# Six gate projections of a retention layer done in the kernel's opening

## The reference

```
mod = (silu(c) @ wmod).reshape(8, 6, 1, 128)
sa, ca, ga, sb, cb, gb = (mod[:, n] for n in range(6))
ga, gb = (sign(a) * maximum(abs(a), 0.25) for a in (ga, gb))
h = layernorm(x) * (1 + ca) + sa
q, k = rotary(h @ Wq.T), rotary(h @ Wk.T)
v, g = h @ Wv.T, h @ Wg.T
o = (q @ k.T / 8 * decay_causal) @ v
o = norm_by_head(o) * gn_weight + gn_bias
x = x + ga * ((o * silu(g)) @ Wo.T)
h = layernorm(x) * (1 + cb) + sb
r = sigmoid(mix(h, mu_r) @ W_r.T)
x = x + gb * r * (relu(mix(h, mu_k) @ W_k.T) ** 2 @ W_v.T)
```

## Time and profile before

| | us |
|---|---|
| median of 3 runs | 756.68 |
| lowest, highest | 756.54, 758.75 |
| span of the profiled execution | 754.3 |
| TensorE busy | 737.0 (98%) |
| VectorE busy | 605.7 (80%) |
| GpSimd busy | 586.0 (78%) |
| ScalarE busy | 489.5 (65%) |

### The profile page before, as it was taken

How to read it: one execution, slowest core, us unless ns; L and a number is a source line. 1 busy time by engine, 2 the same in 40 slices (tenths; PEclk the granted TensorE clock), 3 DMA queues, 4 the chain that set the end, 5 groups by cost and what they waited for, 6 DMA issues and landing times.

```text
span 754.3 us, 29013 instructions
## 1 busy us (share of the span) xinstructions
PE 737.0 (98%) x12148; PEld 647.7 (86%) x12148; DVE 605.7 (80%) x1273; ACT 489.5 (65%) x953; POOL 586.0 (78%) x641
## 2 busy tenths in 40 slices
PE   6999999999999999999999999999999999999987
PEld 5778888888889888988988988888898888888875
DVE  6987787979788787988879798797878878786555
ACT  3576657666675766767566676766666575656664
POOL 2778788888789887898878888788878987776751
PEclk9999999999999999999999999999999999999999
DMA  9320000001011010111102001110101101010000
GB/s 328 102 38 17 16 17 17 16 17 29 10 30 38 9 45 16 24 37 30 31 10 50 17 23 31 27 33 17 44 13 27 38 13 26 16 24 19 22 14 29
DMA packets 56161, 25.67 MB, mean 34 GB/s; under 512 B 36184, under 2 KB 53856, under 8 KB 56032
## 3 DMA queue, kind: packets, MB, share of 16 engines
q1 hardware_dynamic: 55312, 23.02, 12.8%
q10 hardware_dynamic: 720, 0.80, 0.3%
HBM read 11.22 MB, written 4.20 MB: 20 GB/s over the span
## 4 chain that ended last, share of the span: by engine, by line
PE 91%; POOL 2%; issue 2%; DVE 2%; ACT 2%; DMA 0%; POOLq 0%; DVEq 0%
PE ring L309 52%; PE outs L309 15%; PE O_E L309 13%; PE ring L324 8%; PE O_O L309 2%; PE ring L354 2%; POOL qT L1306 0%; POOL gn_rstd L1322 0%; POOL ln_rstd L1278 0%; DMA X<-in_x 0%; ACT y L744 0%; POOL y L1329 0%; ACT y L797 0%; DVE delta L1074 0%; POOL X L1343 0%
## 5 line engine op out<-in xcount | busy, mean ns | idle before, releaser
L1329 POOL TENSOR_TENSOR y<-y,gate 128x512 f32<-128x512 f32 x123 | 158.5, 1304 | 35.7 <-ACT y L744 35.7
L706 ACT ACTIVATE v<-ring 64x512 f32<-64x512 f32 x128 | 76.0, 594 | 81.5 <-PE ring L309 80.7
L309 PEld LDWEIGHTS outs<-wo_gated,y 128*128 128x128 f32 x992 | 119.7, 192 | 6.5 <-POOL y L1329 1.9
L1312 POOL TENSOR_TENSOR rot_k<-rot_k,sin_k 128x256 f32<-128x256 f32 x128 | 106.2, 849 | 24.6 <-DVE sin_k L1025 24.6
L309 PE MATMUL outs<-wo_gated,y 128*128 128x128 f32 x992 | 121.8, 275 | 1.1 <-POOL y L1329 1.0
L1052 DVE TENSOR_REDUCE gn_sum<-N 128x4 f32<-128x512 f32 x118 | 75.5, 681 | 42.4 <-ACT N L732 42.4
L1322 POOL TENSOR_TENSOR gn_rstd<-gn_var,minus_half 128x8 f32<-128x8 f32 x64 | 105.3, 1645 | 5.0
L1306 POOL TENSOR_TENSOR qT<-qT,swapped 128x512 f32<-128x512 f32 x64 | 82.8, 1293 | 28.9 <-DVE swapped L1008 28.9
L1032 DVE TENSOR_TENSOR A<-ring,consts 128x256 f32<-128x256 f32 x128 | 47.9, 414 | 60.0 <-PE ring L309 60.0
L744 ACT ACTIVATE y<-ring,gn 128x512 f32<-128x512 f32 x126 | 90.8, 776 | 5.1 <-PE ring L324 5.1
L714 ACT ACTIVATE kT<-ring 128x512 f32<-128x512 f32 x64 | 38.2, 597 | 77.8 <-PE ring L324 77.8
(11 more groups left out here) (173 smaller groups left out, 2089.4 us busy)
## 6 DMA issues: line engine op xcount, KB each, us to landing
k_odd<-rot_k SPq DMA_DIRECT2D x128, 64.0 KB, 2.4
X<-in_x SPq DMA_DIRECT2D x16, 256.0 KB, 3.7
out<-X SPq DMA_DIRECT2D x15, 256.0 KB, 2.5
key_tables<-in_const SPq DMA_DIRECT2D x7, 256.0 KB, 8.2
rotary_q<-in_const_q SPq DMA_DIRECT2D x2, 512.0 KB, 8.2
gates<-stored_rows SPq DMA_DIRECT2D x8, 128.0 KB, 3.2
N<-in_w_qkT SPq DMA_DIRECT2D x1, 512.0 KB, 4.9
N<-in_w_vT SPq DMA_DIRECT2D x1, 512.0 KB, 6.2
```

The lines of the kernel that those rows point to most:

```text
L309: return e.matmul(o, lhsT, rhs, start=start, stop=stop, skip_group_check=True)
L706: done = e.activation(v[halves(half), i % 2, 1, :, :], by(PAIRS, bank_of["v", odd, i][halves(1 - half), :]), ACT.Copy)
L1312: done = e.tensor_tensor(turned[:, n, :, :], turned[:, n, :, :], sin[:, n, :, :], op)
L1329: e.tensor_tensor(y[:, n % NY, :], y[:, n % NY, :], gate[:, n % 2, :], ALU.mult).then_inc(sem["y"])
```

## The change

The gates of heads 0 to 5 of the first group (`AHEAD_GATES = 6`) are projected in the opening, four where 15 filler matmuls were and two where 7 were. Their banks are `out_bank`, O_E and O_O in turn, which nothing uses yet; `project_gate` waits until the Silu of the gate three before has read its bank. ACT writes the six results into six buffers that stay: the two of `gate`, `delta`, `mix_r` and the two halves of `h2T`, the last four of which belong to the second norm and the mixing and are first used a group later. So that they are not overwritten, `modulate2` and `mix_delta` wait for the sixth y; `mod_gates` and `attend`, which use the three banks, wait for the sixth gate. The split of the gate weights moves forward on ACT (behind that of v) and on POOL (behind the first norm). In the loop the gates begin with number 6, so steps 5 and 6, and the place just ahead of the loop's step 5, lose two each.

```diff
+AHEAD_GATES = 6
+        def gate_buffer(n):
+            ahead = (gate[:, 0, :], gate[:, 1, :], delta[:, :], mix_r[:, :], h2T[:, 0, 1:1 + W], h2T[:, 1, 1:1 + W])
+            return ahead[n] if n < AHEAD_GATES else gate[:, n % 2, :]
...
             def mod_gates():
+                at.wait_ge("gate", AHEAD_GATES)
...
             def attend(i):
+                at.wait_ge("gate", AHEAD_GATES)
...
             def project_gate(n):
-                bank = take_bank(("gate", n), ("gate", n + 1))
+                if n < AHEAD_GATES:
+                    spare = [out_bank[:, :]] + [o[:, :, :].rearrange("p n v -> p (n v)") for o in O]
+                    bank = bank_of["gate", n] = spare[n % len(spare)]
+                    at.wait_ge("gate", n - len(spare) + 1)
+                else:
+                    bank = take_bank(("gate", n), ("gate", n + 1))
                 at.wait_ge("w_g_lo", 1)
+                at.wait_ge("hT_hi", g + 1)
+                at.wait_ge("hT_lo", g + 1)
...
             project_v(0, 1)
-            keep_busy(out_bank, 15, True)
+            for n in range(4):
+                project_gate(n)
             project_v(0, 0)
             transpose_n(1, 0)
             project_k(1)
-            keep_busy(out_bank, 7, True)
+            for n in range(4, AHEAD_GATES):
+                project_gate(n)
...
             project_v(5, 1)
-            project_gate(0)
             project_v(5, 0)
-            project_gate(1)
...
-                for i in due(step - 4, 1, NCHUNK, 1):
+                for i in due(step - 4, 1, NCHUNK, AHEAD_GATES // 2):
                     project_gate(2 * i)
...
             def gate_silu(n):
                 at.wait_ge("gate_psum", n + 1)
-                at.wait_ge(*gated(n - 2))
-                e.activation(gate[:, n % 2, :], bank_of["gate", n][:, :], ACT.Silu).then_inc(sem["gate"])
+                if n >= AHEAD_GATES:
+                    at.wait_ge(*gated(n - 2 if n >= AHEAD_GATES + 2 else n % 2))
+                e.activation(gate_buffer(n), bank_of["gate", n][:, :], ACT.Silu).then_inc(sem["gate"])
...
             def modulate2(g):
                 at.wait_ge("n1T", g + 1)
+                at.wait_ge("y", AHEAD_GATES)
...
             split_w_v()
+            split_w_g()
+            gate_silu(0)
+            gate_silu(1)
             norm_apply(1, 0)
+            gate_silu(2)
+            gate_silu(3)
             copy_v(0, 1)
             copy_v(0, 0)
             round_h(1)
+            gate_silu(4)
+            gate_silu(5)
             copy_kT(0)
-            split_w_g()
...
             def mix_delta(g):
+                at.wait_ge("y", AHEAD_GATES)
...
             norm_rstd(0, 0)
+            split_w_g()
             rotate_q(0)
...
             rotate_k(1)
-            split_w_g()
             rotate_q(4)
```

More of the change, by code:

```diff
@@ L863, in _ @@
             copy_v(5, 1)
-            gate_silu(0)
             copy_v(5, 0)
-            gate_silu(1)
             copy_kT(5)
@@ L878, in _ @@
                     copy_v(i, 1)
-                for i in due(step - 3, 1, NCHUNK, 1):
+                for i in due(step - 3, 1, NCHUNK, AHEAD_GATES // 2):
                     gate_silu(2 * i)
@@ L1328, in gate_head @@
                 at.wait_ge("scaled", n + 1)
-                e.tensor_tensor(y[:, n % NY, :], y[:, n % NY, :], gate[:, n % 2, :], ALU.mult).then_inc(sem["y"])
+                e.tensor_tensor(y[:, n % NY, :], y[:, n % NY, :], gate_buffer(n), ALU.mult).then_inc(sem["y"])
             def mix_delta(g):
```

## The result

| | before | after |
|---|---|---|
| median, run side by side | 756.53 (10 runs) | 760.51 (10 runs) |
| lowest, highest | 756.12, 758.75 | 757.04, 761.25 |
| ratio of after to before | | 1.0037, interval 1.0023 to 1.0051 |
| profiled run: time, span | about 756.2 (the span and 1.9, as in the other profiled runs), 754.3 | 760.85, 759.0 |
| mean granted clock of the profiled run | 0.999 | 0.993 |

The change made the kernel 4.0 us slower. The forecast was 755.0 us in a range of 752.9 to 757.5, with 0.06 for slower. The runs of after order themselves, nearly, by the granted clock: 757.0 and 758.0 us at a mean of 1.00, 758.7 twice at 0.998, 760.4 and 761.3 at 0.996, and 760.6 to 761.2 four times at 0.993.

A forecast was written before the change was run, and what follows sets the result against it. PE was taken as the bound from 65 to 86 us, other engines in the opening. +1.06 (opening), 0 (gates 0, 1) and -2.8 (gates 2 to 5) gave -1.7 us: 755.0 us, range 752.9 to 757.5.

The forecast's parts named there:

- The gain of the two steps without gates 2 to 5: Two steps between 65 and 86 us: four gates leave a full PE, 2.8 us gained.
- Gates 0 and 1 are worth 0: Before `turn_heads(0)`: PE would arrive 1.4 us earlier but wait for DVE's heads, so 0 gained.
- step (c): Opening, ACT: Silus and norm ahead of kT put `scores(0)` 1.06 us late, about 0.9 without the blocking.
- Step (a): Opening: moved wg_lo on POOL blocks DVE's wv_lo, delayed 1.3 us to 18.85; rotation of q ends at 19.0.
- Step (b): Opening, DVE: idle 0.73 us and small gaps absorb most; sin_k, transposes and h_full(1) 0.5 us late.
- In the order of instructions the ring's waits agree again from the ninth step on: After `attend(6)`: everything as before, no lasting change of pace expected.
- Stood in a full PE: Between 65 and 86 us: PE is the bound, so removing gates 2 to 5 gains 4 x 0.70 = 2.8 us.
- the forecast's -1.7: Whole span: +1.06 opening, 0 for gates 0 and 1, -2.8 for gates 2 to 5.
- Rival D: Opening: TensorE falls to 1.2 GHz, `scores(0)` some 5.9 us later, +4.2 in sum, 760.9 us; chance 0.06.

The follow-up runs named there:

- a2: After with seven fillers ahead of v(0, 1), five ahead of `turn_heads(0)` and three behind it; 758.78 us, ratio 1.0028.
- d1: After with one line moved: ACT splits the gate weights before the value weights; 756.78 us, ratio 1.0010.
- b2: Before with gates 0 and 1 made of one matmul each instead of three; 757.49 us, ratio 1.0008.
- c3: After with wv_lo first (DVE), second norm ahead of wg_lo (POOL) and Silus (ACT), gates in a row, fillers, ring's turn passed for gates 0, 1; 756.84 us.
- d2: d1 with second norm ahead of POOL's first rotation and ACT's Silus, gates in a row, fillers, ring's turn passed on for gates 0, 1; 755.83 us.
- b1: Before with only the split of the gate weights (wg_hi, wg_lo) moved forward on ACT and POOL; 757.99 us, ratio 1.0019.
- a3: a2 without the three fillers behind `turn_heads(0)`, the ring's turn passed on wherever a gate was taken out; 758.23 us, ratio 1.0023.
- b3: Before with gates 2 to 5 made of one matmul each instead of three; 755.72 us, ratio 0.9996.
- e1: d2 with POOL's wo_gated moved behind the rstd of the seventh step's heads; 755.30 us, ratio 0.9988.
- a1: After with seven fillers ahead of v(0, 1); 761.14 us, ratio 1.0050.
- c1: After with DVE's wv_lo ahead of its first q rotation; 758.11 us, ratio 1.0013.

## Why the prediction was wrong

**What held.** The gain of the two steps without gates 2 to 5: 2.8 forecast, 2.87 in a2 at full clock. Gates 0 and 1 are worth 0: PE waits 1.40 us for DVE's N in their place (after; 1.41 in d1), b2 gains nothing, and with the turn passed on step 4 is 9.55 and 9.69 us (c3, d2) against 9.68. wg_lo from 15.35 (15.42), wv_lo's end at 18.85 (18.90), v(0, 1) at 19.0 (19.04).

ACT's first Silus and the norm stood in a2 where step (c) put them, at 20.71, 21.41 and 21.90.

**Step (a), "the rotation of q ends at 19.0".** It ends at 20.04. I applied the exclusion to wv_lo and forgot it for POOL's instruction that starts while wv_lo stands and then runs. By the Trainium skill (SBUF — State Buffer, section Who interferes with whom) whoever issues first has the shared ports for its whole instruction, and the other blocks fully. The traces agree, in after, b1 and c3 (wv_lo 2.48 and 2.08 us for 1.21, a rotation 2.27 for 1.30, a small instruction 1.28 for 0.19); applied to both engines in turn the rule gives the end of b1's rotation to 0.2 us (wv_lo's end at 18.75 and 1.30 more, against 19.89).

**Step (b), "sin_k, the transposes and h_full(1) are 0.5 us late".** They are 1.3 late. The 0.73 us idle before 21.69 was no slack: DVE waited there for POOL, and POOL was late by the same amount. Terms (a) and (b) were sized 0.5 and are 1.33 (0.9 to 1.2 in b1, 0 in d1).

**Step (c)** was forecast as 0.9 without the blocking, and is 0.54 in d1. In sum the opening at full clock is +1.9 (a2), against 1.06; the 0.8 between them are what (a) and (b) lack. "PE's gates 4 and 5 end at about 27.0 and are not the last wait" holds at full clock (a2, where ACT's kT is last) and not in after, where PE is.

**"In the order of instructions the ring's waits agree again from the ninth step on, so I expect no lasting change of pace".** They differ before it. The change of turn puts sin_k(6) ahead of `transpose_k(5)`: +1.07 us in step 4 of a2, 1.03 of them between `turn_heads(0)` and attend(4), and gone in a3, c3 and d2, which pass the turn on. Step 7 takes 0.77 back: where gates 2 to 5 have left the ring and its turn is not kept, it is 11.3 to 11.5 us, and in b3 and a3 it is 10.74. The change of turn does most of that as well. It puts sin_k(9) ahead of `transpose_k(8)`, which then follows `turn_heads(3)` by 1.03 to 1.26 us, where in before, a3, b1, b2 and b3 it follows by 0.55. The rest, 0.17 in after, lies ahead of `turn_heads(3)` (9.95 us from attend(6), against 9.78) and is absent in c3, d2 and e1. e1's earlier gn_rstd takes 0.21 off the wait for sin_k (1.24 to 1.03).

**"Stood in a full PE".** The reason was not right, so the right size was luck. b3 and a3 show that PE's work alone is worth 0.5 us. The rest came from the banks, whose new turn takes the wait for sin_k out of steps 5 and 6.

These make the forecast's -1.7 a +0.9, to 0.1 us what a2 has (+0.87): 0.8 in the opening, 1.07 in step 4, 0.77 in step 7. After's two runs at full clock lie 0.5 and 1.4 us above before's median.

**Rival D, given 0.06, is the rest of the 4 us.** "Against it: the granted clock stays at 1.00 through the 0.95 us idle before 23.68" was too weak an argument for an idle time of 1.78 us. Its price was wrong as well: 0.95 us in the opening (after against a2), not 5.9. PE was back at the full clock at 22.94, so seven matmuls of the gates took the extra time and not all the 7.9 us of work. Their delay went to ACT's Silus, norm and copies of v, hence to `project_k(1)` (27.12 against 25.77), and 0.4 us of it was absorbed because a2's `scores(0)` waits for kT. Two more falls did the rest. The one at `turn_heads(0)` lies in steps 4 and 5: step 5 is 10.04 us where a2 has 8.92, so 1.1 us. The one near 740 us lies in

```profile
740.00:742.00 2.00, 2.00 (x8) 1.71 (x8) 0.00 (x0) 0.66 (x2) 0.00 (x0) 0.50 0.04 8
742.00:744.00 2.00, 2.00 (x23) 1.71 (x23) 0.00 (x0) 0.77 (x2) 0.00 (x0) 0.68 0.00 0
```

and is worth 1.5 us of the span (+3.16 to +4.7). Nothing of the change is there. The chain has the same waits in both profiles: after is 3.17 us behind at the three matmuls behind mix_k_lo (736.58 and 739.75) and 4.71 behind at the next matmul of the chain (744.61 and 749.32). Before has a fall at the end too, but in its last microseconds, where little is left for PE; so have a1, a2 and d2, and a3 has it earlier, as after.

That the change brings falls about is shown by the runs, for all of them together: of the 108 runs of before that were timed beside the experiments, none has a mean clock below 0.998, and six of after's ten have 0.993 to 0.996. It isn't shown for the fall near 740 us. Fifteen of those 108 runs have 0.998 and take 758.0 to 759.2 us, some 2 us above the others, so a fall or two happens in before as well; which, no trace shows. What decides whether the clock falls at a given idle time stays open too: behind 1.78 us in after it fell, behind 1.40 in b1 it did not; behind 1.55 us ahead of the transposes it fell in a1 and not in a2; and at `turn_heads(0)` it fell behind 1.40 us in after and not behind 1.41 in d1, 1.64 in a1 and 1.65 in c1.

## What to carry to other kernels

When a two-input DVE instruction is moved beside GpSimd work, follow the blocking through in both directions, the next instruction of the one that blocked included, and move the newcomer to a place where one of the two is idle: here one line of ScalarE's order was worth 3.7 us in the median, some 1 us by the blocking and the rest with the clock falls. An engine at 100% is not by itself the bound, if its buffers come round by a turn: make the work cheaper in place, and see whether the step gets shorter, before its removal is priced. Where work is taken out of a ring of buffers, all later takes get other banks, so read the new waits at each step up to where they agree again, and not only from there on: here two steps lost a late wait and two others got one.

## What the runs showed of the hardware

- A DVE instruction with two inputs in SBUF and a POOL instruction beside it exclude each other, and by turns: wv_lo 2.48 for 1.21 us behind wg_lo, then a rotation 2.27 for 1.30 behind wv_lo. A 128x4 instruction of POOL took 1.28 us in place of 0.19 beside wv_lo. DVE's instructions with one input in the ring, and its shuffle, took their usual 0.68 and 0.74 us beside wg_lo.
- The block shows as length and not as idle time: neither the wv_lo of 2.48 us nor the rotation of 2.27 has an idle time or a releaser in front. The mean duration of its kind is what gives it away.
- An idle time of PE that the profile puts down to "issue" (0.77 us before 67.84, 0.38 before 98.52) was a wait whose end agrees to 0.1 us with that of DVE's sin_k.
- The runs of one program, after, differ by 4 us of 760 with their mean clock: 757.04 us at 1.00, 760.4 to 761.3 at 0.993 to 0.996. One fall near 740 us, with the same waits around it, cost 1.5 us.
